# Second buffers for the later stages, one x2 tile per pair, and a new written-out order of all engines' steps, in a four-stage image kernel on one core

## What is computed

```python
x = _L0_conv_ref(x, ...)   # channel attention: softmax(q k^T / 8) v, plus x
x = _L1_conv_ref(x, ...)   # 3x3 deformable convolution: offsets and masks from a convolution,
                           # bilinear samples, batch norm, relu
x = _L2_conv_ref(x, ...)   # pixel attention (256 x 256), projection, plus x
x = _L3_conv_ref(x, ...)   # layer norm, 3x3 depthwise, four gated 5-tap scans, fuse, plus x;
                           # layer norm, gated two-layer product, plus x
```

## Time and profile before

| what | value |
|---|---|
| time of the runs | 303.65 us median of 3 (303.65, 303.65, 304.49) |
| profiled execution: span | 301.8 us, 7399 instructions |
| profiled execution: own whole time | not listed apart; the median lies 1.85 us above the span |
| PE busy | 95% of the span |
| DVE, ACT, POOL busy | 71%, 63%, 18% |
| chain that ended last | PE 85%, DVE 5%, ACT 5%, issue 3% |
| granted TensorE clock | 9 (90% or more) in all 40 slices |

### The profile page before, as it was taken

One profiled execution on the slowest core, in us unless ns is written; L12 is line 12 of the kernel. 1 busy time (PEld: TensorE's weight loads), 2 busy tenths in 40 slices (PEclk: granted clock), 3 DMA queues, 4 the chain that ended last, 5 costly groups with the idle time before them and its releaser, 6 DMA issues.

```text
span 301.8 us, 7399 instructions
## 1 busy us (share of the span) xinstructions
PE 287.8 (95%) x2870; PEld 183.7 (61%) x2870; DVE 213.0 (71%) x424; ACT 190.4 (63%) x399; POOL 53.0 (18%) x139
## 2 busy tenths in 40 slices
...
DMA packets 3057, 4.98 MB, mean 16 GB/s; under 512 B 336, under 2 KB 2768, under 8 KB 2896
## 3 DMA queue, kind: packets, MB, share of 16 engines
...
## 4 chain that ended last, share of the span: by engine, by line
PE 85%; DVE 5%; ACT 5%; issue 3%; POOL 1%; ACTq 0%; POOLq 0%; DVEq 0%
PE ps_cv L534 22%; PE ps_pair L615 11%; PE ps_yb L494 8%; PE ps_pair L480 7%; PE ps_ma L437 6%; PE ps_ma L464 4%; PE ps_mb L580 3%; PE ps_pair L602 3%; PE ps_pair L570 3%; PE ps_mb L591 3%; PE ps_mb L547 3%; PE ps_mb L388 2%; PE ps_pair L635 2%; PE ps_mb L624 2%; PE ps_yb L374 1%
## 5 line engine op out<-in xcount | busy, mean ns | idle before, releaser
L901 DVE TENSOR_TENSOR sb_wt<-ps_yb,sb_xe 128x512 f32<-128x512 f32 x144 | 94.0, 684 | 26.4 <-PE ps_xb L489 24.9
L534 PE MATMUL ps_cv<-sb_wt,sb_w_x 128*64 128x256 f32 x576 | 77.3, 385 | 0.0
L740 ACT ACTIVATE sb_xe<-ps_xb 128x512 f32<-128x512 f32 x72 | 43.0, 597 | 19.3 <-PE ps_xb L489 19.2
L534 PEld LDWEIGHTS ps_cv<-sb_wt,sb_w_x 128*64 128x64 f32 x576 | 38.2, 136 | 20.2 <-issue 7.5
L615 PE MATMUL ps_pair<-sb_y_pad,sb_par 64*128 64x256 f32 x320 | 37.4, 383 | 0.3 <-ACT sb_gates L799 0.3
L615 PEld LDWEIGHTS ps_pair<-sb_y_pad,sb_par 64*128 64x128 f32 x320 | 30.9, 184 | 5.8 <-issue 2.5
L942 DVE SCALAR_TENSOR_TENSOR sb_dw_acc<-sb_z_pad,sb_par,sb_dw_acc 128x256 f32<-128x256 f32 x56 | 25.2, 480 | 9.4 <-ACT sb_dw_acc L792 5.3
L494 PE MATMUL ps_yb<-sb_hats,sb_sel 32*128 32x512 f16 x144 | 29.8, 383 | 0.7
L1039 POOL TENSOR_TENSOR sb_parts<-sb_hat,sb_parts 128x256 f16<-128x256 f32 (+2 forms) x40 | 23.3, 615 | 38.7 <-ACT sb_parts L710 38.6
L1046 POOL TENSOR_SCALAR sb_sc<-sb_mv 128x1 f32<-128x1 f32 x16 | 3.0, 190 | 142.1 <-DVE sb_mv L936 74.7
L489 PE MATMUL ps_xb<-sb_hats,sb_sel 32*128 32x512 f16 x72 | 27.7, 385 | 0.2 <-ACT sb_hats L719 0.2
...
## 6 DMA issues: line engine op xcount, KB each, us to landing
...
```

Source lines behind the costliest of these rows:

```text
L534: mm = nc.tensor.matmul(cv[C * b:C * (b + 1), 0:PIX], w_x[n % 2][:, b, h, k, :], wt_of(n, k, h)[:, PIX * b:PIX * (b + 1)], start=(k == 0 a ...
L740: nc.scalar.activation(xe[t % XE][:, :], xb[:, :], ACT.Copy).then_inc(ev("xe_ok"), 1)
L901: nc.vector.tensor_tensor(wt_of(n, k, h)[:, :], yb[h][:, :], xe[t % XE][:, :], ALU.mult)\
```

## The change

`PLAN` is written anew for all four engines. Each engine's list has the same steps as before, in another order; PE's has one more, `hot.10`. `WARM` stays as it is, `HOT` sums to 25 passes in place of 46. `x2` has eight tiles, `x4` three, and the single buffers of the later stages two. The waits over them go from `n - 1` to `n - 2`, and some 20 steps on ACT and DVE get a wait before the overwriting of a buffer that had none written out. Two more memsets stand on DVE at the start. The diff, cut:

```diff
     "pe": """
-        warm.1 warm.2 qk.1 attn.1 warm.3 at.1 warm.4 mix.1 x1.1 warm.5 off.1 prep.1 off_t.1 qk.2 wx0.1 attn.2 warm.6
-        warm.7 qk.3 wx2.1 at.2 wx1.1 mix.2 tr0.1 x1.2 sp_first.1 tr1.1 attn.3 sp0.1 wx2.2 tr2.1 s0a.1 sp1.1 off.2 sp2.1
-        at.3 off_t.2 s0b.1 s1a.1 sp3.1 wx0.2 s1b.1 s2a.1 mix.3 sp4.1 s2b.1 s3a.1 s3b.1 x1.3 sp5.1 s4a.1 qk.4 s4b.1 sp6.1
-        wx1.2 tr0.2 sp7.1 s5a.1 s5b.1 s6a.1 attn.4 sp8.1 tr1.2 s6b.1 s7a.1 s7b.1 at.4 tr2.2 sp0.2 off.3 s8a.1 s8b.1
...
-        s5a.8 s5b.8 s6a.8 sp7.8 ff.5 et1.7 sp8.8 s6b.8 gate.6 et0.7 sp_last.8 s7a.8 av.7 s7b.8 s8a.8 s8b.8 ff2.5 scan.6
-        qk2.8 hot.1 logit.8 fuse.6 hot.2 hot.3 v2.8 hot.4 et0.8 gate.7 et1.8 av.8 scan.7 hot.5 ff.6 fuse.7 gate.8 hot.6
-        scan.8 ff2.6 hot.7 fuse.8 ff.7 hot.8 ff.8 ff2.7 hot.9 ff2.8
+        warm.1 warm.2 warm.3 warm.4 qk.1 warm.5 warm.6 attn.1 warm.7 at.1 mix.1 x1.1 off.1 prep.1 off_t.1 qk.2 attn.2
+        wx0.1 qk.3 wx2.1 at.2 mix.2 tr0.1 wx1.1 sp_first.1 tr1.1 x1.2 sp0.1 attn.3 tr2.1 sp1.1 s0a.1 off.2 sp2.1 wx2.2
+        at.3 s0b.1 off_t.2 s1a.1 sp3.1 wx0.2 s1b.1 s2a.1 s2b.1 mix.3 s3a.1 sp4.1 wx1.2 x1.3 sp5.1 s3b.1 qk.4 s4a.1 sp6.1
+        s4b.1 tr0.2 s5a.1 attn.4 sp7.1 wx2.3 s5b.1 tr1.2 s6a.1 s6b.1 sp8.1 at.4 s7a.1 tr2.2 s7b.1 mix.4 sp0.2 off.3
...
+        s4b.8 s5a.8 s5b.8 s6a.8 sp7.8 ff.5 s6b.8 s7a.8 sp8.8 et1.7 gate.6 et0.7 sp_last.8 s7b.8 av.7 s8a.8 s8b.8 ff2.5
+        scan.6 qk2.8 hot.1 logit.8 v2.8 hot.2 fuse.6 hot.3 et0.8 gate.7 et1.8 hot.4 av.8 scan.7 hot.5 ff.6 hot.6 gate.8
+        fuse.7 hot.7 scan.8 ff2.6 hot.8 fuse.8 ff.7 hot.9 ff.8 ff2.7 hot.10 ff2.8
     "act": """
-        attn.1 at.1 mix.1 off.1 prep.1 tanh.1 abs.1 attn.2 wx0.1 high.1 wx2.1 at.2 wx1.1 mix.2 tr0.1 xe0.1 tr1.1 xe1.1
-        tr2.1 wx2.2 xe2.1 attn.3 halve.1 off.2 at.3 xe3.1 xe4.1 abs.2 mix.3 tanh.2 wx0.2 xe5.1 high.2 xe6.1 xe7.1 xe8.1
...
+        attn.1 at.1 mix.1 off.1 prep.1 tanh.1 abs.1 attn.2 wx0.1 high.1 at.2 wx2.1 mix.2 tr0.1 xe0.1 tr1.1 xe1.1 tr2.1
+        xe2.1 wx1.1 attn.3 off.2 wx2.2 xe3.1 xe4.1 abs.2 at.3 tanh.2 wx0.2 mix.3 xe5.1 high.2 xe6.1 wx1.2 xe7.1 tr0.2
...
     "dve": """
-        st1.7 out.5 dw3.7 dw5.7 dw2.7 dw4.7 dw6.7 dw8.7 prod.6 dw7.7 max.8 x4.6 nrm0.8 y.7 nrm1.8 st2.6 x3.8 st1.8 dw2.8
-        dw3.8 dw4.8 dw5.8 dw6.8 prod.7 dw7.8 dw8.8 y.8 u.6 x4.7 st2.7 out.6 prod.8 x4.8 st2.8 u.7 out.7 u.8 out.8
...
+        dw2.7 dw4.7 dw3.7 dw5.7 dw6.7 dw7.7 prod.6 dw8.7 y.7 max.8 x4.6 nrm0.8 nrm1.8 st2.6 x3.8 st1.8 dw3.8 dw2.8 dw4.8
+        dw5.8 dw7.8 dw6.8 dw8.8 y.8 prod.7 u.6 x4.7 st2.7 out.6 prod.8 x4.8 st2.8 u.7 out.7 u.8 out.8
     "pool": """
-        x1.1 grid.1 bn.1 low.1 x1.2 low.2 x1.3 x1.4 low.3 ln1.1 low.4 ln1.2 x1.5 ln2.1 low.5 ln1.3 x1.6 ln2.2 low.6
+        grid.1 x1.1 low.1 x1.2 low.2 x1.3 bn.1 low.3 x1.4 ln1.1 low.4 ln1.2 x1.5 low.5 ln2.1 ln1.3 x1.6 ln2.2 low.6
...
-HOT = {1: 4, 2: 2, 3: 3, 4: 2, 5: 5, 6: 5, 7: 8, 8: 13, 9: 4}
+HOT = {1: 2, 2: 1, 3: 3, 4: 1, 5: 3, 6: 3, 7: 1, 8: 4, 9: 4, 10: 3}
 WARM = {1: 5, 2: 2, 3: 5, 4: 1, 5: 3, 6: 2, 7: 3}
...
-        x2 = [sb(f"x2{i}", [P, PIX]) for i in range(3)]
+        x2 = [sb(f"x2{i}", [P, PIX]) for i in range(PAIRS)]
...
-        z_pad = sb("z_pad", [P, H + 2, PW])
+        z_pad = [sb(f"z_pad{i}", [P, H + 2, PW]) for i in range(2)]
...
             def attn(n):
+                wait_past(act, ev("a_nrm_ok"), n - 1)
                 act.wait_ge(ev("a_neg_ok"), n)
...
             def ln1(n):
                 act.wait_ge(ev("h1_ok"), n)
-                wait_past(act, ev("y_ok"), n - 1)
+                wait_past(act, ev("y_ok"), n - 2)
...
             def dw_sum(n):
-                wait_past(dve, ev("gate_mm"), n - 1)
-                wait_past(dve, ev("scan_mm"), n - 1)
+                wait_past(dve, ev("gate_mm"), n - 2)
+                wait_past(dve, ev("scan_mm"), n - 2)
...
             def prod_step(n):
+                wait_past(dve, ev("fuse_mm"), n - 2)
                 dve.wait_ge(ev("gate_ok"), n)
...
-            nc.vector.memset(z_pad[:, :, :], 0.0).then_inc(zero_ok, 1)
-            nc.vector.memset(y_pad[:, :, :], 0.0).then_inc(zero_ok, 1)
+            for i in range(2):
+                nc.vector.memset(z_pad[i][:, :, :], 0.0).then_inc(zero_ok, 1)
+                nc.vector.memset(y_pad[i][:, :, :], 0.0).then_inc(zero_ok, 1)
```

More of the change, by code:

```diff
@@ L60 @@
[L60 to L74, removed]
```

192 lines of the change are left out of this document (111 added, 81 removed).

## The result

The changed kernel took **306.5 us** (median of 4 runs, 305.86 to 307.07) where the kernel before took 304.07 beside it: ratio 1.0082, 95% interval 1.0059 to 1.0105. It is slower, by about 2.5 us; the prediction said 302.4 in a range of 300.2 to 305.4. The profiled execution took 306.63 with a span of 304.8 (before: 301.8), at a mean granted clock of 0.983.

The account below looks back on a forecast made before the run. PE, busy 95% of the span, was taken to bound the kernel, with single chains at both ends. Start +0.7, middle -2.2 and end +0.3 summed to -1.2: span 301.8 to 300.6, median 302.4, range 300.2 to 305.4.

Parts of the forecast that it names:

- The middle: 33 to 255 us: the new order covers PE's load waits and wins all visible idle time, -2.2 us, bounds -5.7 and +2.2.
- The waits named: Middle: PE's weight loads waited 3.1 us for `xe`, 1.3 for `w`, 1.3 for `mix`; these get cover.
- Under 1 us idle: Middle: sign that the forecast is right, PE idling under 1 us between 33 and 255 us.
- The failed step: Start: PE busy 3.86 of 6.40 us without a clock fall, used as argument against the clock rival at the end.
- the wait at `qk.1`: Start: 13 zero passes ahead of the first real product, with those behind, delay the chain 1.5 us, bounds 0.55 and 2.6.
- Part of it comes back at `tr0.1`: Start: earlier copy of the hats recovers 1.2 us; late `wx2.2` loses 0.6, a filled wait at `off_t.2` saves 0.2.
- I take 0; at the most some ten of them stand in pair 8's chain: Some 20 added waits, already met, cost 0; at 0.05 us each, bounded at 0.5 in pair 8's chain.
- The end: Pair 8's chain: DVE doing `dw8.7` and `y.7` ahead of `max.8` costs +0.3 us, bounds 0 and 1.0.
- So 0: End: the 21 `HOT` passes removed, 4.5 to 4.8 us of PE, all lay inside waits, so no time changes.
- The rival of the clock: End: fewer passes let the clock fall to 1.2 GHz ahead of `ff.8`, costing 1.4 us, total 303.8; chance 0.05.
- The rival that ended slower, by the wait at `qk.1`: Start: zero passes delay everything behind `qk.1` while the middle returns less than the start loses; 305.4 us, chance 0.19.

Follow-up runs that it names:

- before_warm_moved: Kernel before with only the start's zero passes at the changed kernel's places (13 ahead of qk.1, none later than at.1); 306.7 us, ratio 1.0092.
- before_hot_25: Kernel before with 22 zero passes at the end (its label says 25) in place of 46, order and start unchanged; 304.38 us, ratio 1.0027.

## Why the prediction was wrong, step by step

**The middle** had the right size, in part by luck. Forecast -2.2 from the new order; the new order and buffers without the added waits give 221.66 less 219.24 to 219.34, so -2.3 to -2.4; the added waits take 0.6 to 0.8 back, and -1.69 is left. The waits named went as forecast. But -2.2 was to be all of PE's visible idle time, and that is not where it came from: PE's idle time between `sp3.1` and `s8b.8` fell only from 2.18 to 1.60, and the other 1.1 us came out of its busy time, 219.48 to 218.37 for the same products, which fits the loads that no longer wait for `xe`. "Under 1 us idle" was missed.

**The failed step** is in the start: "Against it: from 6.1 to 12.5 us PE was busy only 3.86 of 6.40 us and the granted clock stayed 1.00". The clock was made a rival at the end alone, and the passes taken out of the first chain's gaps were costed as cover of nothing: the prediction weighed what they delay at their new place and not what they did at the old one. That row was no proof. The changed kernel was busy 4.56 of 6.83 us from 5.59 to 12.42, a larger share, and the clock fell behind it. What differs is the end of the stretch: in the last 3.17 us ahead of `x1.1` PE was busy 0.91 us, with only `at.1` and `mix.1` between its waits; in the kernel before it was 1.56, with `warm.4` and a part of `warm.3` (`warm.5` stands behind `x1.1`). That is not all of it: the profile of `before_warm_moved` has the same 0.91 of 3.17 and no fall, and its clock had first risen at 3.84 us, not at 5.59. What decides between these two stays open. The fall made 2.6 of the 3.73 lost up to `qk.2`; the rest is the wait at `qk.1`, 1.12 by `attn.1` (forecast 1.5, bounds 0.55 to 2.6).

The Trainium skill, "TensorE: Matmul & The Clock Gate" (Part 1: The HAM clock gate), calls the throttled state the default, with activity as what releases it. The falls at 12.42 and 299.14 agree with it in kind, both behind stretches with gaps, though ahead of the first no idle time is longer than 0.88 us. The prediction cited this for the end only.

**"Part of it comes back at `tr0.1`"**, -0.8 net: nothing came. From `qk.2` to `sp3.1` all kernels of the new order take 17.03 to 17.26, before 17.19. The copy of the hats did come earlier, 8.17 us behind `qk.2` for 8.83 before, and by `sp3.1` it was lost again, with `x1.2` and `wx2.2` put behind the copy.

**"I take 0; at the most some ten of them stand in pair 8's chain"**: 1.1 to 1.2 us in all. The 0.4 to 0.5 of it at the end lie just within the bound of 0.5 for pair 8's chain, and 0.05 us a wait, for which the prediction named no row, was near the 0.06 measured. The 0.6 to 0.8 in the middle had neither a term nor a bound. The evidence for the 0 was a row where waits are hidden, two `w` products running back to back on a busy DVE; a wait on an engine that stands idle for its data is not hidden, and the chain has such places in every pair. What the doubled buffers cost by themselves doesn't show in the new order's stretches; that order with single buffers was not tried, so what they give there is open.

**The end**, +0.3 by DVE's order: +0.45 came, but from the waits; the order is worth 0.1. **`HOT`**, "So 0": 0.47 in this profile, 0.8 in the kernel before by `before_hot_25`. The rival of the clock had the right mechanism, and the place right in `before_hot_25`; in the changed kernel it came 1.4 us after `ff.8` had begun and cost a third of the 1.4.

The rival that ended slower, by the wait at `qk.1` (305.4), had the sign and about 1.1 of its cause; the middle that it wanted empty was not.
